# First projection moved up among the token tiles, its stacks moved in halves, and narrow score rows in four banks

## The reference

```python
h = hot_vec if is_hot else cold_lat @ proj_w.T       # token table, 8000 hot rows, 24000 cold rows
qkv = layernorm(h) @ w_project.T                     # 16 heads of 32
att = softmax(causal(q @ k.T / sqrt(32))) @ v
h = h + att @ w_out.T
h = h + experts(layernorm(h), top 2 of 16) + shared_expert(layernorm(h))
```

## Time and profile before

| | us |
|---|---|
| median of 3 runs (1026.65 to 1028.84) | 1027.39 |
| profiled execution, its own time | 1029.54 |
| its span | 1027.7 |
| PE busy | 939.7 (91%) |
| DVE busy | 665.9 (65%) |
| ACT busy | 601.4 (59%) |
| POOL busy | 313.0 (30%) |

### The profile page before, as it was taken

The page is one execution under the profiler, slowest core; times in us unless marked ns, Lnnn a source line. Parts: engine busy times, 40 slices in busy tenths (PEclk is TensorE's granted clock), DMA queues, the critical chain, the costliest instruction groups (busy, mean ns, idle before and its releaser), DMA issues.

```text
span 1027.7 us, 21178 instructions
## 1 busy us (share of the span) xinstructions
PE 939.7 (91%) x6811; PEld 684.8 (67%) x6811; DVE 665.9 (65%) x1746; ACT 601.4 (59%) x1306; POOL 313.0 (30%) x320
## 2 busy tenths in 40 slices
PE   6677599999999999999998889899989999999992
PEld 5333458678686867768686678777866666666661
DVE  8975356566675756667576857757866666666660
ACT  7212167777777767677777832231146777777770
POOL 2287210110202011020202005633344377246542
PEclk9679889999999999999999999999999999999996
DMA  6132824151343406233345021171449768845553
GB/s 217 37 90 86 195 59 107 33 123 43 83 114 67 99 4 133 63 83 84 71 96 186 23 84 62 62 287 51 166 144 339 202 123 179 269 89 95 94 70 41
DMA packets 44574, 114.39 MB, mean 111 GB/s; under 512 B 9332, under 2 KB 11380, under 8 KB 42162
## 3 DMA queue, kind: packets, MB, share of 16 engines
q1 hardware_dynamic: 32146, 87.14, 29.2%
q0 software_dynamic: 12320, 25.90, 13.7%
HBM read 53.03 MB, written 25.17 MB: 76 GB/s over the span
## 4 chain that ended last, share of the span: by engine, by line
PE 71%; issue 8%; DVE 7%; DMA 5%; POOL 4%; ACT 3%; POOLq 0%; another core or an unknown queue 0%; ACTq 0%; DVEq 0%
PE psum L528 11%; PE psum L1349 10%; PE psum L498 8%; PE psum L541 7%; PE psum L518 7%; PE psum L1424 6%; PE psum L503 6%; PE psum L1289 5%; DMA out<-xnT,slot_out 4%; PE psum L1273 3%; PE psum L1393 2%; PE psum L1371 2%; PE psum L544 2%; DVE oh_lo L1585 1%; ACT probsT L595 1%
## 5 line engine op out<-in xcount | busy, mean ns | idle before, releaser
L652 DVE CUSTOM_DVE_ANT_0 psum<-psum,mask_row 128x128 f32<-128x128 f32 (+7 forms) x256 | 194.3, 763 | 59.4 <-PE psum L518 57.0
L610 ACT ACTIVATE probs<-psum,nmax 128x128 f32<-128x128 f32 (+7 forms) x256 | 190.4, 744 | 48.6 <-DVE nmax L652 42.7
L528 PE MATMUL psum<-ident,probs 128*128 128x128 f32 x1152 | 172.6, 275 | 4.7 <-ACT probsT L595 3.2
L518 PE MATMUL psum<-k_stack,q_stack 128*128 128x512 f32 (+2 forms) x384 | 155.0, 459 | 19.0 <-issue 9.2
L528 PEld LDWEIGHTS psum<-ident,probs 128*128 128x128 f32 x1152 | 136.1, 140 | 37.0 <-issue 19.0
L595 ACT COPY probsT<-psum 128x512 f32<-128x512 f32 (+3 forms) x256 | 129.0, 504 | 38.0 <-PE psum L528 33.4
L498 PE MATMUL psum<-xnT,w_unit 128*128 128x512 f32 x256 | 131.4, 603 | 0.2 <-ACT full L473 0.2
L445 POOL CAST part_hi<-full 128x512 fp32r<-128x512 f32 x32 | 19.6, 612 | 352.2 <-ACT full L473 247.4
L878 POOL DMA_INDIRECT out<-xnT,slot_out x47 | 82.5, 1756 | 110.6 <-DMA out<-xnT,slot_out 75.8
L518 PEld LDWEIGHTS psum<-k_stack,q_stack 128*128 128x128 f32 x384 | 68.5, 201 | 64.1 <-ACT probs L610 40.9
L1424 PE MATMUL psum<-w_dn,gated_T 128*128 x188 | 88.6, 594 | 1.7 <-ACT gated_T L932 1.7
(11 more groups left out here) (242 smaller groups left out, 1849.6 us busy)
## 6 DMA issues: line engine op xcount, KB each, us to landing
w_gu<-in_wgu SPq DMA_DIRECT2D x16, 1024.0 KB, 7.9
q_stack<-part_hi SPq DMA_DIRECT2D x64, 128.0 KB, 2.4
q_stack<-part_lo SPq DMA_DIRECT2D x64, 128.0 KB, 2.4
k_stack<-part_hi SPq DMA_DIRECT2D x64, 128.0 KB, 2.4
k_stack<-part_lo SPq DMA_DIRECT2D x64, 128.0 KB, 2.4
w_dn<-in_wd SPq DMA_DIRECT2D x16, 512.0 KB, 10.0
out<-acc SPq DMA_DIRECT2D x17, 256.0 KB, 3.7
hot_all<-xn SPq DMA_DIRECT2D x4, 1024.0 KB, 7.9
```

The source lines that it names most:

```text
L518: mm = pe.matmul(dst[:, c0:c1], qs, k_stack[b][:, h, c0:c1], start=True, stop=True)
L528: mm = pe.transpose(bank(4 + m % 2)[:, (j - 4 * k) * P:(j - 4 * k + 1) * P], probs[n % PSLOTS][:, j * P:(j + 1) * P], ident[:, :])
L610: act.activation(probs[n % PSLOTS][:, 0:(i + 1) * P], bank(2 * (n % 2), 2)[:, 0:(i + 1) * P], ACT.Exp, bias=nmax[:, n % 4:n % 4 + 1], scal ...
L652: dve.tensor_tensor_reduce(out=row, in0=row, in1=mask_row[:, (QT - 1 - i) * P:QT * P], scale=1.0, scalar=3.0e38, op0=ALU.add, op1=ALU.min, ...
```

## The change

- `LAG` is 2: POOL computes the inverse deviation of tile c - 3 after the gathers of tile c.
- Only 11 of the 16 lookups stand ahead of the token loop (`EARLY_LOOKS`). The other five stand in it, at c = 1 to 5, on PE and on DVE, with their `row_numbers`. Their bank for odd tiles is 7.
- The fills of unit 0 stand at c = 7, 8, 9, 11, 12, 13, in the order q first half, k first half, v first half, q second half, k second half, v second half.
- For them, `full` and POOL's split are gone: ACT writes the high part straight from bank 7 (`first_high`) and DVE the low part (`first_low`). The next fill waits for the low part.
- SP moves the stacks of unit 0 in halves of 512 columns (`first_stack`): q first half behind the store of h tile 7, k first half behind the store of h tile 8, the second halves behind the store of tile 15. That is 64 transfers instead of 32, each of half the size. The first scores wait for the first halves alone, the scores of step 16 for the second.
- ACT, DVE and SP wait for the stores of all h tiles before attention.
- In steps 0 to 15 of a unit, where a row of scores has at most 512 columns, each step has one bank, n % 4. The scores of step n + 2 are issued in step n and wait for the exponential of step n - 2. The first two score rows of a unit are issued together at the end of the unit before. From step 16 on all is as before.

```diff
-LAG = 4
+LAG = 2
+EARLY_LOOKS = 11
+FIRST_FILL = {7: 0, 8: 2, 9: 4, 11: 1, 12: 3, 13: 5}
-FILL0 = NT // BATCH + 3
...
+        NARROW = STEPS // 2
+
+        def score_bank(n):
+            return bank(n % 4) if n < NARROW else bank(2 * (n % 2), 2)
...
+        def first_stack(sp, side, half):
+
+            cols = slice(half * 512, half * 512 + 512)
+            st = (q_stack, k_stack)[side][0]
+            sp.wait_ge(s_lo, HEAD + 2 * half + side + 1)
+            for r in range(4):
+                low = r % 2 if side == 0 else r // 2
+                src = part_lo if low else part_hi
+                for h in range(GH):
+                    sp.dma_start(st[32 * r:32 * r + 32, h, cols].bitcast(F32),
+                                 src[32 * h:32 * h + 32, side, cols].bitcast(F32)).then_inc(s_first[half], 16)
...
+        def look_bank(c):
+            return bank(4 if c % 2 == 0 else 5 if c < EARLY_LOOKS else 7)
...
+        def first_high(act, c):
+
+            f = FIRST_FILL[c]
+            n = list(FIRST_FILL.values()).index(f)
+            side, half = f // 2, f % 2
+            cols = slice(half * 512, half * 512 + 512)
+            act.wait_ge(s_fill, HEAD + n + 1)
+            if side == 0:
+                act.activation(part_hi[:, 0, cols], bank(7), ACT.Copy, scale=-ATT_SCALE).then_inc(s_hi, 1)
+            elif side == 1:
+                act.copy(part_hi[:, 1, cols], bank(7)).then_inc(s_hi, 1)
+            elif half == 0:
+                act.copy(v_unit[0][:, 0:4, :].rearrange("p a n -> p (a n)"), bank(7)).then_inc(s_fact, 1)
+
+        def first_low(dve, c):
...
+            if side < 2:
+                dve.wait_ge(s_hi, HEAD + 2 * half + side + 1)
+                if side == 0:
+                    dve.scalar_tensor_tensor(out=part_lo[:, 0, cols], in0=bank(7), scalar=-ATT_SCALE,
+                                             in1=part_hi[:, 0, cols].bitcast(F32), op0=ALU.mult,
+                                             op1=ALU.subtract).then_inc(s_lo, 1)
...
+        def first_piece(pe, c):
+
+            f = FIRST_FILL[c]
+            pe.wait_ge(s_w, 16)
+            pe.wait_ge(s_xC, 4 * (f % 2) + 4)
+            if f == 0:
+                pe.wait_ge(s_looked, 2 * NT)
+            elif f == 1:
+                pe.wait_ge(s_fact, HEAD + 3)
+            else:
+                pe.wait_ge(s_lo, HEAD + {2: 1, 4: 2, 3: 3, 5: 4}[f])
...
-                pe.wait_ge(s_E, HEAD + u * STEPS + n - 1)
-                dst = bank(2 * (n % 2), 2)
+                if n < 2:
+                    pe.wait_ge(s_E, HEAD + u * STEPS - 1)
+                elif n < 4:
+                    pe.wait_ge(s_E, HEAD + u * STEPS)
+                elif n < NARROW:
+                    pe.wait_ge(s_E, HEAD + u * STEPS + n - 3)
+                elif n == NARROW:
+                    pe.wait_ge(s_E, HEAD + u * STEPS + n - 2)
+                else:
+                    pe.wait_ge(s_E, HEAD + u * STEPS + n - 1)
+                dst = score_bank(n)
...
-                    if n + 1 < STEPS:
+                    if u == 0 and n + 1 == STEPS // 2:
+                        pe.wait_ge(s_first[1], STACKED)
+                    if n + 2 < NARROW:
+                        scores(u, b, n + 2)
+                    elif NARROW <= n + 1 < STEPS:
                         scores(u, b, n + 1)
-                    elif nxt:
+                    elif n + 1 == STEPS and nxt:
                         first_scores(u + 1, 1 - b, g + b)
...
-                if c == NT - LAG:
-                    stack(sp, 0, 0, (0,), first=True)
-            stack(sp, 0, 0, (1,), first=True)
+                if c in (7, 8):
+                    first_stack(sp, c - 7, 0)
+            for side in range(2):
+                first_stack(sp, side, 1)
+            sp.wait_ge(s_hst, 16 * NT)
...
+            for c in range(EARLY_LOOKS):
+                look_up(c)
+                if c % PER == PER - 1:
+                    row_numbers(c // PER)
             for c in range(NT + 1):
+                if c in FIRST_FILL:
+                    first_low(dve, c)
                 if c < NT:
                     embed(c)
                 if c >= 1:
                     norm(c - 1)
-                if 0 <= c + 1 - FILL0 < FILLS:
-                    fill_evac(dve, "dve", 0, c + 1 - FILL0, 0)
+                if 1 <= c <= NT - EARLY_LOOKS:
+                    look_up(EARLY_LOOKS + c - 1)
+                    if (EARLY_LOOKS + c) % PER == 0:
+                        row_numbers((EARLY_LOOKS + c) // PER - 1)
+            dve.wait_ge(s_hst, 16 * NT)
```

More of the change, by code:

```diff
@@ L402, in load_w, with stack @@
                          a["wqkv"][bass.ds(g, 1), :, :, :].rearrange("o p k n -> (o p) k n")).then_inc(s_w, 16)
-        def stack(sp, u, b, sides=(0, 1), first=False):
-            if not first:
-                sp.wait_ge(s_S, HEAD + (u - 1) * STEPS)
-            for side in sides:
+        def first_stack(sp, side, half):
[8 more added lines that the diff above has]
+                                 src[32 * h:32 * h + 32, side, cols].bitcast(F32)).then_inc(s_first[half], 16)
+        def stack(sp, u, b):
+            sp.wait_ge(s_S, HEAD + (u - 1) * STEPS)
+            for side in range(2):
                 st = (q_stack, k_stack)[side][b]
@@ L440, in split_part @@
             pool.wait_ge(s_fact if side == 0 else s_fdve, HEAD + 3 * u + half + 1)
-            if loaded is not None:
+            if u == 1:
+                pool.wait_ge(s_first[half], STACKED)
+            else:
                 pool.wait_ge(s_stack[1 - b], loaded)
@@ L571, in first_scores @@
                 scores(u, b, 0)
+                scores(u, b, 1)
             first_scores(0, 0, 0)
@@ L1518, in _ @@
                 inv_std(pool, c)
-                if c < NT - 1:
-                    half = c - NT + LAG + 1
-                    split_part(pool, 0, 0, half // 2, half % 2, None)
             att_pool(pool)
@@ L1700, in _ @@
                           skip_group_check=True).then_inc(s_look, 1)
+            for c in range(EARLY_LOOKS):
+                look(c)
             pe.wait_ge(s_proj, 16)
```

67 lines of the change are left out of this document (42 added, 25 removed).

## The result

The changed kernel takes **1010.93 us** (median of 4 runs, 1010.23 to 1011.66); the kernel before took 1028.12 in the runs beside it (4 runs, 1026.65 to 1029.29). The ratio is 0.9838, 95% interval 0.982 to 0.9855. The forecast was 1011.3 with 1006.5 to 1018. The profiled execution took 1011.66, with a span of 1009.9 us where before it was 1027.7.

The account below looks back on a forecast made before the run. PE was taken to bound the kernel (71% of the chain), with a wait for the stacks before attention. First scores 11.7, clock 2.1 and narrow rows 2.3 sum to 16.1 us: 1027.39 becomes 1011.3, range 1006.5 to 1018.

Parts of the forecast that it names:

- The first scores: Token stage: attention's first scores come at 115.9 instead of 127.58, 11.7 us earlier; bounds 8.6 and 13.5.
- adds no work to POOL: Token stage: `LAG` of 2 costs POOL nothing extra; the deviation need only be ready when tile c's gathers are issued.
- The clock: Unit 0, steps 3 to 16: the low granted clock costs 2.1 us, all taken as gained; bounds 0 and 2.1.
- if PE stands still for one or two us instead of nine, I expect no fall: Ahead of the first scores: with a shorter PE standstill the granted clock stays up, gaining 2.1 us.
- the rival with 0.18: Around the first scores: the clock falls all the same, giving 1013.4 us; chance 0.18.
- The narrow rows: Steps 0 to 15 of units: fewer PE waits for exponentials, 2.3 us gained; bounds 0.8 lost and 6.4 gained.
- I take 1.9 us, nearly all: Units 0 to 6: of 2.3 us that PE waits for exponentials at the scores, 1.9 is gained.
- the wait mostly moves: Unit 7's narrow half: the wait goes from scores to transposes, so only 0.4 us of 4.5 is gained.
- The pieces: Stacks of unit 0: half pieces take 0.32 to 0.645 us; second halves land about 128, at most 134.0, needed at 135.7.
- It is the moving that costs, not the issue: Stack transfers: full DMA engines set the 0.645 us of a whole piece, so half a piece takes 0.32 to 0.645.
- The rival of dear pieces: Stacks: half pieces cost 0.98 us each, PE waits 9.1 us before step 16, total 1020.4 us; chance 0.09.
- The sum: Whole kernel: 11.7 + 2.1 + 2.3 = 16.1 us gained, from the median 1027.39 to 1011.3 us.

Follow-up runs that it names:

- looks16: The changed kernel with all 16 lookups ahead of the first tile again, instead of 11 ahead and 5 between tiles: 1015.83 us, ratio 0.9866.
- the filled hole: The kernel before with 72 transposes of the identity in PE's 9.15 us standstill ahead of the first scores: 1024.5 us, ratio 0.9984.
- tail_v: The changed kernel with the sixth fill cut into four pieces, laid into rounds 13 to 16: 1007.17 us, ratio 0.98; run again, 1006.7 us, ratio 0.9811.
- narrow_only: The kernel before with only the narrow score rows in four slots, the token stage unchanged: 1024.76 us, ratio 0.9957.
- quarter_pieces: The changed kernel with the stacks' second halves in 64 pieces of 32 x 256 instead of 32 of 32 x 512: 1030.49 us, ratio 1.0017.

## Why the prediction came out right

- **The first scores** (11.7 forecast, 12.45 measured). First fill at 72.50 for 72.7, sixth at 100.77 for 100.4, tile 15 summed at 110.01 for 109.6: the chain is right at each link. The last copy ended at 115.07, where I took 115.9 for stalls that did not come in full. I had the place of the lookups right (`looks16`: 2.6 us), but **the sentence that `LAG` "adds no work to POOL" missed what it does**: with 4 the first fill comes 5.8 us later, and the whole takes 4.4 us more by the ratios, 6.1 in the medians.
- **The clock** (2.1 forecast, 1.00 won). Two steps failed. The price was too low: taken from unit 1's 20.3 us it came to 2.1, the filled hole shows 2.70. Of the missing 0.6, half lies in steps 0 to 2, which the sum left out though the clock is low there too (127.58 to 129.53, 1.95 us, against 1.67 from 126.60 to 128.27); the rest is that steps 3 to 16 at the full clock take 18.10 (128.27 to 146.37) and not the 18.4 taken from unit 1. And **"if PE stands still for one or two us instead of nine, I expect no fall" is wrong**: it fell, for 6.8 us, with no gap above 1.6 us ahead of it (PE busy 5.77 us of 9). My argument against this rival, that PE keeps the full clock from 87 to 119 "though it has gaps", was weak: in that window PE is busy 30.04 us of 32. What exactly makes the clock fall stays open: filling the gaps held it in one trace, but `tail_v` fell in one execution and not in the other with the same gaps. This was the rival with 0.18; its condition was met, and it took 1.1 of the 2.1 us, since the low stretch was 6.8 us and not 13.7.
- **The narrow rows** (0.27 a unit and 0.4 in unit 7 forecast; 0.10, with 0.46 in unit 0, and 1.24 in unit 7's narrow half measured, 0.95 in the whole unit). The step that failed is "I take 1.9 us, nearly all": the exponentials' waits went, 2.3 us, but the transposes then wait 1.1 us more for DVE's copies, and a unit is only 0.10 shorter. In unit 7 "the wait mostly moves" is what the rows show, but I had sized it from nothing. In `narrow_only` unit 7's narrow half gained only 0.3 and the whole unit nothing (57.56 both times), in an execution where one copy of DVE there took 0.67 us instead of 0.23; whether that copy is the reason is not shown.
- **The pieces.** "It is the moving that costs, not the issue" is wrong. Whole pieces filled the DMA engines and took 0.645 us, and I took the one for the cause of the other; pieces of half and of a quarter the size cost as much, 0.63, with the engines less than half busy. What saved the number is that the sum was also made with 0.645 as the upper bound: landed by 134.0 was foreseen, 134.19 measured, needed at 136.14. The margin is 2 us, not the 7.7 that I took. The rival of dear pieces had the kind right (a price that does not fall with size) and the size wrong. The figure of 0.95 us for 64 KB that I quoted from the Trainium skill (DMA: Bandwidth & Descriptors, section Bandwidth) is for loads from HBM that GpSimd issues. Here the sync queue's 64 KB pieces within SBUF follow each other at 0.63 to 0.74.
- **The sum** (16.1; 16.1 to the end of unit 7's narrow half, 17.2 in the medians). That the time fits to 0.4 us is partly luck, twice over. The terms cancel: 0.75 too little for the stage and 0.8 for unit 7 stand against 1.1 too much for the clock and 0.5 for units 0 to 6. And the gain in the medians is 1.1 us more than forecast, of which 0.7 vanish because the kernel before came out at 1028.12 and I had counted from 1027.39.

## What to carry to other kernels

Before you cut a transfer to start it earlier, ask which of two limits it sits on, and bound it with the price of a whole one: a queue that issues back to back pays per piece, so twice the pieces can cost all the gain (`quarter_pieces`). When a long serial block holds up a stage that another engine bounds, cut it and lay the pieces into that engine's rounds; here that brought the first scores 3.7 us forward (`tail_v`), and in one of two profiled executions the clock did not fall. And a stall that you remove is not the only thing that lowers the clock: look at the granted clock in the part that must run fast, and if it is low, try to fill PE's gaps just ahead of it, with useful work or without. Judge that by several runs, since one and the same kernel can do either.

## What the runs showed of the hardware

- Copies from 32 partitions of SBUF to 32 others, issued by the sync queue, mostly follow each other at 0.63 to 0.645 us for 128, 64 and 32 KB; some stretches took 0.69 to 0.74 (64 KB) and 0.98 (128 KB). GpSimd's own come at 0.51 us for 64 KB, and with both queues at work the rate was 203 GB/s instead of 120.
- The same kernel ran between 104 and 150 us with no low clock in one execution and with 7 us of it in another, where it costs 2.75 us, after the same 8 us of PE (busy 6.15 in both).
- The clock fell without a long stand-still: in the changed kernel PE was busy 5.77 of the 9 us from 104 to 113 and idle in three gaps of 0.7 to 1.6 us. In the one trace with these filled to 7.85 it did not fall.
- The part behind attention, the same work in every kernel, took 422.7 to 426.4 us in the profiled executions.
